# Target scores in single-pass fp32r with rounded copies of keys and queries, and router products of 8 columns

## The reference, cut to what matters

```python
def attention(src, tgt, src_mask, tgt_mask, W_src, b_src, W_tgt, b_tgt, W_out, b_out):
    k, v = split((src @ W_src.T + b_src) * src_mask[:, :, None])   # 8 heads of 16
    q = (tgt @ W_tgt.T + b_tgt) * tgt_mask[:, :, None]
    scores = einsum('bthd,bshd->bhts', q, k) / sqrt(16)
    scores = where(src_mask[:, None, None, :] == 0, -inf, scores)
    attn = softmax(scores, axis=-1)
    upd = einsum('bhts,bshd->bthd', attn, v).reshape(b, t, 128)
    return concatenate([tgt, upd], axis=2) @ W_out.T + b_out

def ffn(x, router_w, w1, w2):                   # 4096 tokens, 8 experts
    probs = softmax(x @ router_w.T)
    topv, topi = top_k(probs, 2);  topv /= topv.sum(-1, keepdims=True) + 1e-9
    cw = (one_hot(topi, 8) * topv[..., None]).sum(axis=1)
    y = gelu(x @ w1[e]) @ w2[e]                 # for each expert e
    return (cw * y).sum over the experts

x = x + tanh(g_xattn) * attention(ctx, layernorm(x), mask, mask, ...)
x = x + tanh(g_ffn) * ffn(layernorm(x), ...)
```

## Time and profile before

| | |
|---|---|
| median of 3 runs | 340.66 us (340.45 to 340.8) |
| profiled execution | 339.91 us |
| its span on the core | 338.1 us, 10971 instructions |
| busy, share of the span | PE 88%, PEld 79%, DVE 63%, ACT 57%, POOL 60% |

### The profile page before, as it was taken

How to read it: one execution, slowest core, us unless ns; L and a number is a source line. 1 busy time by engine, 2 the same in 40 slices (tenths; PEclk the granted TensorE clock), 3 DMA queues, 4 the chain that set the end, 5 groups by cost and what they waited for, 6 DMA issues and landing times.

```text
span 338.1 us, 10971 instructions
## 1 busy us (share of the span) xinstructions
PE 297.4 (88%) x3633; PEld 266.6 (79%) x3633; DVE 214.0 (63%) x909; ACT 192.4 (57%) x472; POOL 202.1 (60%) x267
## 2 busy tenths in 40 slices
PE   1989999999999999997949997998999999999910
PEld 1777777787877878785738987998999999999910
DVE  2457577679888887889657796335843433335553
ACT  3166757868686886867685437546444444444300
POOL 3433233243586877857464788878878865655750
PEclk9999999999999999999998999999999999999985
DMA  7525521213042211751143222311452432248346
GB/s 226 154 85 168 162 92 33 80 37 95 25 116 69 61 54 49 225 162 31 49 109 94 65 69 83 81 47 55 105 120 87 132 102 72 64 137 286 98 127 187
DMA packets 41237, 34.61 MB, mean 102 GB/s; under 512 B 5044, under 2 KB 36950, under 8 KB 41184
## 3 DMA queue, kind: packets, MB, share of 16 engines
q1 hardware_dynamic: 33152, 23.62, 25.1%
q0 software_dynamic: 4320, 8.47, 7.0%
q10 hardware_dynamic: 3712, 1.84, 1.9%
HBM read 22.35 MB, written 12.01 MB: 102 GB/s over the span
## 4 chain that ended last, share of the span: by engine, by line
PE 72%; DVE 8%; issue 6%; ACT 5%; DMA 4%; POOL 3%; SPq 1%; POOLq 0%; ACTq 0%; DVEq 0%
PE ps_sc L1554 18%; PE ps_proj L1567 9%; PE ps_o L1567 8%; PE ps_o L1513 4%; PE ps_proj L1442 4%; PE ps_proj L1445 3%; PE ps_sc L1395 3%; PE ps_sc L1407 3%; PE ps_sc L1390 3%; PE ps_tail L1498 2%; PE ps_xT L1436 2%; ACT xr L772 2%; PE ps_tail L1489 2%; PE ps_proj L1459 2%; PE ps_o L1454 1%
## 5 line engine op out<-in xcount | busy, mean ns | idle before, releaser
L653 POOL DMA_INDIRECT picked<-yo,xg x71 | 72.2, 1016 | 16.5 <-issue 11.9
L1554 PE MATMUL ps_sc<-xt,w1c 128*128 128x128 f32 x568 | 76.3, 278 | 1.2 <-ACT xt L795 0.9
L635 POOL DMA_INDIRECT rows<-xr,posi x64 | 63.4, 990 | 18.0 <-issue 18.0
L1554 PEld LDWEIGHTS ps_sc<-xt,w1c 128*128 128x128 f32 x568 | 69.9, 194 | 2.2 <-ACT xt L795 1.3
L804 ACT ACTIVATE probT<-ps_sc 128x512 f32<-128x512 f32 x71 | 42.4, 597 | 43.8 <-PE ps_sc L1554 43.8
L1188 DVE TENSOR_REDUCE rowmax<-ps_sc 128x4 f32<-128x512 f32 x64 | 43.6, 690 | 24.8 <-PE ps_sc L1411 20.6
L698 ACT ACTIVATE probT<-ps_sc,pencol 128x512 f32<-128x512 f32 x64 | 43.6, 683 | 20.5 <-PE ps_sc L1411 18.3
L583 POOL TENSOR_TENSOR kblk<-kT,headcol 128x256 f32<-128x256 f32 x32 | 19.7, 614 | 54.3 <-ACT kT L730 54.1
L1567 PE MATMUL ps_proj<-w2s,probT 128*128 x288 | 38.5, 277 | 0.0
L1567 PE MATMUL ps_o<-w2s,probT 128*128 x280 | 37.0, 275 | 0.0
L1306 DVE COPY w1c<-w1s 128x512 f32 x71 | 31.4, 445 | 7.8 <-issue 2.8
(11 more groups left out here) (164 smaller groups left out, 587.2 us busy)
## 6 DMA issues: line engine op xcount, KB each, us to landing
xg<-rows SPq DMA_DIRECT2D x71, 65.0 KB, 1.8
ctxs<-ctxT SPq DMA_DIRECT2D x32, 128.0 KB, 2.1
xs<-x SPq DMA_DIRECT2D x8, 256.0 KB, 3.0
maskbc<-mask SPq DMA_DIRECT2D x8, 256.0 KB, 4.0
w1s<-w SPq DMA_DIRECT2D x4, 512.0 KB, 3.9
w2s<-w SPq DMA_DIRECT2D x8, 256.0 KB
maskbc<-picked SPq DMA_DIRECT2D x4, 512.0 KB, 6.6
out<-xs ACTq DMA_DIRECT2D x6, 256.0 KB, 2.3
```

The lines of the kernel that those rows point to most:

```text
L635: nc.gpsimd.indirect_dma_start(out=rows, out_offset=bass.IndirectOffsetOnAxis(ap=posi[:, i, pick, b:b + 1], axis=0), in_=xr[:, i, pick, b, ...
L653: nc.gpsimd.indirect_dma_start(out=picked, out_offset=bass.IndirectOffsetOnAxis(ap=xg[:, r, D + 1:D + 2].bitcast(I32), axis=0), in_=yo[:, ...
L1554: last = nc.tensor.matmul(ps_score[j % DEEP][:, c * 128:(c + 1) * 128], w1c[:, j % DEEP, c * 128:(c + 1) * 128], xt[:, j % XRING, :], star ...
```

## The change

Two new buffers, both of type fp32r: `kblkr` (as `kblk`) and `qTr` (as `qT`). The target scores are multiplied from them, in fp32r, in place of `qT` and `kblk` in fp32. The source scores stay as they were. POOL writes `kblkr` with a second instruction like L583, ahead of it. ACT writes `qTr` with a copy of `qT`, after the far exponential and ahead of L724 and `kT`. PE waits for `kblkr` and `qTr` ahead of the target scores, and for `kblk` ahead of the source scores, one step later than before. ACT's write of `kT` waits for both of POOL's products of the sequence four before. Apart from that the router products stream 8 columns each.

```diff
+        kblkr = sb("kblkr", [128, KQ, PAIR, T], F32R)
+        qTr = sb("qTr", [128, KQ, T], F32R)
@@ POOL, step
                     wait(pool, s_sc, n - 2)
                     nc.gpsimd.tensor_tensor(
+                        kblkr[:, r, :, :], kT[:, r, :].unsqueeze(1).broadcast_to([128, PAIR, T]),
+                        headcol[:, :].unsqueeze(2).broadcast_to([128, PAIR, T]), ALU.mult).then_inc(s_kblkr, 1)
+                    nc.gpsimd.tensor_tensor(
                         kblk[:, r, :, :], kT[:, r, :].unsqueeze(1).broadcast_to([128, PAIR, T]),
                         headcol[:, :].unsqueeze(2).broadcast_to([128, PAIR, T]), ALU.mult).then_inc(s_kblk, 1)
@@ ACT, step
                     exponent(n, FAR, far_heads, s_exp)
+                n = sequence(g, k, LAG_SCORE)
+                if n is not None:
+                    act.wait_ge(s_q, n + 1)
+                    wait(act, s_sc, n - 3)
+                    nc.scalar.activation(qTr[:, n % KQ, :], qT[:, n % KQ, :], ACT.Copy).then_inc(s_qr, 1)
...
                     act.wait_ge(s_proj, n + 1)
+                    wait(act, s_kblkr, n - 3)
                     wait(act, s_kblk, n - 3)
@@ PE, score_block
                     pe.wait_ge(s_maxT, m + 1)
+                    pe.wait_ge(s_kblk, m + 1)
...
-                    pe.wait_ge(s_kblk, n + 1)
-                    pe.wait_ge(s_q, n + 1)
+                    pe.wait_ge(s_kblkr, n + 1)
+                    pe.wait_ge(s_qr, n + 1)
...
-                        nc.tensor.matmul(scores[:, j, TARGET], qT[strip, n % KQ, :], kblk[strip, n % KQ, :, :],
+                        nc.tensor.matmul(scores[:, j, TARGET], qTr[strip, n % KQ, :], kblkr[strip, n % KQ, :, :],
                                          start=m is None, stop=False, skip_group_check=True)
@@ PE, step
-                        last = nc.tensor.matmul(ps_tail[:, b * 128:(b + 1) * 128], x2nT[:, b, :],
-                                                router, start=True, stop=True)
+                        last = nc.tensor.matmul(ps_tail[:, b * 128:b * 128 + EXPERTS], x2nT[:, b, :],
+                                                router[:, 0:EXPERTS], start=True, stop=True)
```

More of the change, by code:

```diff
@@ L361, in gated_cross_attention_moe @@
         s_kblk = sem("s_kblk")
+        s_kblkr = sem("s_kblkr")
+        s_qr = sem("s_qr")
         s_sc = sem("s_sc")
```

## The result

The changed kernel took 344.39 us (median of 10 runs, 342.12 to 345.29), the kernel before 340.73 beside it. The ratio is 1.0116, with a 95% interval of 1.0083 to 1.0148: the change made the kernel slower, by some 4 us. Forecast were 339.1 us, a gain of 1.6.

A forecast was written before the change was run, and what follows sets the result against it. POOL's nearly full list up to group 3's last scatter was taken as the bound: 1.94 from target scores - 0.2 ACT copy - 0.15 POOL gave 1.6 us off 340.66, so 339.1 us; range 337.2 to 341.1.

The forecast's parts named there:

- the second product on POOL: POOL from (5, 1) to group 3's last scatter: 15 x 0.59 = 8.85 us against 8.7 of waits, 0.15 over.
- Target scores: On PE, fp32r takes away one of two rounds: 0.215 us a sequence, bounds nothing and 0.32.
- its nine: Steps up to the keys of (5, 1) counted as passing on the shorter target scores: 9 x 0.215 = 1.94 us.
- the bf16 rate: Rival on PE: fp32r streams 256 columns as bf16, 0.32 us a step, gain 2.5, 338.2 us; chance 0.17.
- no saving: Rival on PE: 256 fp32r columns take as long as two fp32 instructions, only costs remain, 341.0 us; chance 0.14.
- The copy on ACT: Query copy ahead of kT: 0.2 us, hidden in ACT's wait except at k = 1 from g = 4 on.
- the router: Router products with 8 columns still load 128 columns of weights: 0 us gained a group, bounds 0 and 0.89.
- What counts is what is gained by (5, 1): Attention gains count only by bringing POOL's last scatter of group 3 forward; POOL's list begins 1.74 us earlier at (5, 1).
- while POOL sets the end this adds nothing: DVE's L1253, waiting for POOL's addition L620, stalls at (7, 0) and (8, 0), at no added time.
- Waits for keys that are still there: Sign of being wrong: POOL's waits for keys from (5, 1) on remain, so ACT or DVE held the steps.
- PE is ahead of that: Between last scatter and slots: PE has gained more by then, and the slots wait for the load.
- The one that ended slower: Rival: the rounded copy costs POOL 0.85 us a product, end 2.3 us later, 343.0 us; chance 0.16.

The follow-up runs named there:

- e1: Kernel before plus a second POOL product behind kblk that nobody reads; PE, ACT and router as before: 348.25 us, ratio 1.0268.
- e11: Kernel before plus ACT's copy of the queries alone, which nobody reads: 339.73 us, ratio 0.9996.
- e3: Kernel before with router products of 8 columns and nothing else: 339.53 us, ratio 0.9980.
- e2: Changed kernel with one POOL product: only kblkr is written, and the source scores read it as fp32: 337.94 us, ratio 0.9967.
- e4: Changed kernel with second POOL product, ACT's copy and fp32r scores only for the first 17 sequences: 339.31 us, ratio 1.0014.
- e8: Changed kernel with POOL writing kblkr alone, no ACT copy, DVE writing queries as fp32r; source scores read both as fp32: 336.65 us, ratio 0.9886.
- e9: Changed kernel with idle PE products, four and six, in two waits of step (9, 0): 341.65 us, ratio 1.0068.
- e6: Changed kernel with DVE's integer copy L994 moved behind the addition to x in the attention steps: 341.62 us, ratio 1.0027.

## Why the prediction was wrong

The step that failed is the second product on POOL: it was priced on POOL's own list alone, at 0.15 us more than POOL's waits would hide. It holds up DVE, and by itself it made the kernel before 2.7% slower (e1).

*Target scores: right in kind, 0.30 instead of 0.215 a step.* L1421's own stretch is the 0.21 us expected of one round. The rest came from L1409 ahead of it, whose stretch fell from 0.50 to 0.42. Why that one shortened the runs do not show. From (2, 0) to (5, 1) eight steps gave 0.30 each, where the text counted seven of its nine: k = 2 did shorten, in g = 2, 3 and 4, which it had named as a sign of being wrong, while (2, 3) and (4, 0) did not. The 0.21 also rules out the rivals of the bf16 rate (0.11) and of no saving (0.43).

*The copy on ACT and the router: right, with some luck.* The copy is busy 304 ns and sets `kT` back by 0.20 (84.42 to 84.62 in (5, 1)), and e11 shows 0.9996. But the keys of (5, 1) came 0.48 later in their step, since the near exponential had to wait for DVE's maxima behind the shorter scores. That POOL's list still began 1.87 us earlier, where 1.74 was said, is because PE had gained 2.35 and not 1.94: two misses that nearly cancel. L1512's stretch fell from 0.89 to 0.81, and e3 shows nothing.

*What counts is what is gained by (5, 1): nearly right for the scatter, where little disturbs DVE.* In e2 and e4 the scatter moved by 2.48 and 2.27 us, and (5, 1) by 2.48 and 2.35; in e8 by 3.12 and 2.52.

*The second product on POOL: the step that failed.* Its own price, 614 ns, was right. But the text took POOL's 8.7 us of waits as free room for 15 of them, and of DVE's late L1253 it said that "while POOL sets the end this adds nothing". The changed kernel's waits of POOL, from (5, 1) to the scatter:

```profile
POOL kblkr L587 <- ACT kT L743: 8.5, 5, 3.7
POOL rs L606 <- DVE ve L860: 0.4, 2, 0.2
```

Without the 3.7 ahead of its start 5.2 us of waits are left, and the list is 164.27 - 85.58 = 78.69 us long, where 73.86 + 0.15 was said. POOL became full only at the end of the list, behind (8, 2), where one more product costs 0.57; before that the steps grew longer. Waits for keys that are still there were among the text's own signs of being wrong, and it named ACT or DVE for them: it was DVE. In e1, 4.60 of the 4.75 us lost by (8, 3) are steps in which `tw` was held. The waits that looked free were those in which DVE came through. The trace of before had the rows to see it in, shown above: `tw` and the copy, each ending with an instruction of POOL.

*"PE is ahead of that": wrong.* PE's tail ran at a clock of 0.50 up to 172 us and set the first slot, 5.76 us later than before, while the loads were issued only 0.94 later. With the clock at 1.00, in e9, the first slot came 3.25 us earlier.

*The rivals.* The one that ended slower priced the product on POOL itself at 0.85 us; it took 0.61. Slower it was, but by DVE and the clock, a mechanism that no case had.

*Which instructions were held.* Among them were the copy of 8 integers (2.52 us), `nm` beside a memset (1.47), and `tw`, which has two inputs (2.34). Which one is caught depends on what stands there: L994 in the changed kernel, `tw` in e1, L1007 and L1028 in e6. A start ahead of POOL's did not save it: the copy's row begins at 99.22, and POOL's addition, which began at 99.87, still went first.

## What to carry to other kernels

Before work is put into an engine's idle time, look who lives in that time: on POOL, go through DVE's short SBUF instructions and see whether they end just behind POOL's (0.02 to 0.03 us here). When an operand is needed rounded, and its other readers can bear that, let the instruction that writes it anyway round it (e8), before a second copy is made. And when PE gets faster, see what it then waits for, since a wait can cost twice, in itself and in the clock after it: here waits of 1.08 and 1.48 us stood ahead of a tail of 11.87 us, at a clock of 0.50 up to 172 us, where at 1.00 it took 8.66 (e9).

## What the runs showed of the hardware that was not expected

A DVE instruction stayed held over three POOL instructions in a row, with at most 0.03 us between them (scatter, addition, product; 2.52 us), and the scatter held it too: the copy began 0.62 us ahead of the scatter's end and did not come through. What let it through in the end, though the next product began at 101.67, the runs do not show. Ten idle PE products (1.00 and 1.34 us) in two waits of the changed kernel brought the first slot 3.25 us forward: in that execution the clock was 1.00 behind them, up to the first slot.
